# Three pieces of work put in another order in the attention loop of a one-core attention and mixture-of-experts kernel

## The reference

```python
def reference(x, ctx_1024, g_xattn, g_ffn, ...):       # x, ctx: (32, 512, 512)
    x = x + tanh(g_xattn) * xattn(layernorm(x), ctx, ctx, ...)
    x = x + tanh(g_ffn) * ffn(layernorm(x), ...)

def xattn(q, k, v, ...):                               # 8 heads of 64
    gi = concatenate([q, k, v], axis=-1)
    ig, fg = gi @ igate_w.T + igate_b, gi @ fgate_w.T + fgate_b     # by head and row
    cs = cumsum(log_sigmoid(fg))
    log_D = where(tril, cs[:, None] - cs[None, :], -inf) + ig[None, :]
    D = exp(log_D - max(log_D))
    C = (qh @ kh.T / sqrt(64)) * D
    h = (C / (maximum(abs(C.sum(-1)), exp(-max(log_D))) + 1e-6)) @ vh
    return (h - mean(h)) / sqrt(var(h) + 1e-5) * out_w              # by head

def ffn(x, ...):     # 8 experts, each takes its 2048 likeliest of 16384 rows
    ...
```

## Time and profile before

| | us |
|---|---|
| median of 3 runs | 3043.23 (3041.03 to 3049.25) |
| profiled execution, its own time | 3042.49 |
| its span, first to last instruction | 3040.7 |
| mean granted TensorE clock | 0.986 of 2.4 GHz |
| busy in the span: PE, DVE, ACT, POOL | 2903.3, 1824.0, 1073.1, 1064.0 |
| first stage, to the first instruction of the selection | 988.3 |

### The profile page before, as it was taken

How to read it: one execution, slowest core, us unless ns; L and a number is a source line. 1 busy time by engine, 2 the same in 40 slices (tenths; PEclk the granted TensorE clock), 3 DMA queues, 4 the chain that set the end, 5 groups by cost and what they waited for, 6 DMA issues and landing times.

```text
span 3040.7 us, 59653 instructions
## 1 busy us (share of the span) xinstructions
PE 2903.3 (95%) x24196; PEld 2342.4 (77%) x24196; DVE 1824.0 (60%) x5124; ACT 1073.1 (35%) x1897; POOL 1064.0 (35%) x1029
## 2 busy tenths in 40 slices
PE   6999999999997599999999999999999999999998
PEld 5777777777776477877877777787787787777886
DVE  6999999999997745344454444445535445444332
ACT  4777777777775211121211121122112112112110
POOL 4778777777785311211112111121112112121111
PEclk8999999999998799999999999999999999999999
DMA  5355554555543412231232132232123114222121
GB/s 176 130 196 175 190 183 168 197 185 179 195 163 113 127 34 38 56 75 31 54 95 51 31 80 38 37 100 55 34 36 98 35 33 110 37 51 57 35 37 24
DMA packets 157977, 284.18 MB, mean 93 GB/s; under 512 B 32992, under 2 KB 32992, under 8 KB 157704
## 3 DMA queue, kind: packets, MB, share of 16 engines
q1 hardware_dynamic: 123704, 204.36, 20.1%
q0 software_dynamic: 28672, 67.65, 12.6%
q10 hardware_dynamic: 5328, 8.36, 0.9%
HBM read 170.79 MB, written 101.19 MB: 89 GB/s over the span
## 4 chain that ended last, share of the span: by engine, by line
PE 63%; DMA 2%; DVE 2%; issue 0%; ACT 0%; POOL 0%; ACTq 0%; DVEq 0%; POOLq 0%
PE DN L1736 32%; PE UP L1707 30%; DMA w_raw<-in_L_ffn_W_down 2%; PE TT L1680 1%; DVE c_hit L1399 0%; DVE down_lo L1265 0%; PE c_bank L1392 0%; ACT z L1650 0%; PE c_bank L1376 0%; DVE c_hit L1420 0%; DVE c_within L1415 0%; ACT down_hi L1259 0%; POOL out_x L1625 0%; DVE mid_lo L1768 0%; DVE c_gained L1452 0%
## 5 line engine op out<-in xcount | busy, mean ns | idle before, releaser
L1625 POOL DMA_INDIRECT out_x<-y,slots x128 | 208.5, 1629 | 1622.3 <-DVE y L1792 1622.3
L1650 ACT ACTIVATE z<-UP,bup 128x512 f32<-128x512 f32 (+1 forms) x352 | 240.7, 686 | 1082.1 <-PE UP L1707 1060.5
L1736 PE MATMUL DN<-down_hi,mid_hi 128*128 128x512 f32 x1408 | 570.9, 405 | 0.0
L1707 PE MATMUL UP<-xT_hi,up_hi 128*128 128x512 f32 (+1 forms) x1408 | 553.8, 393 | 2.3 <-DVE xT_lo L1747 1.2
L1707 PE MATMUL UP<-xT_hi,up_lo 128*128 128x512 f32 (+1 forms) x1408 | 554.7, 394 | 0.0
L1707 PE MATMUL UP<-xT_lo,up_hi 128*128 128x512 f32 (+1 forms) x1408 | 551.4, 392 | 0.0
L1736 PE MATMUL DN<-down_hi,mid_lo 128*128 128x512 f32 x1280 | 505.8, 395 | 0.0
L1736 PE MATMUL DN<-down_lo,mid_hi 128*128 128x512 f32 x1280 | 505.7, 395 | 0.0
L1766 DVE CAST mid_hi<-z 128x512 fp32r<-128x512 f32 (+1 forms) x352 | 151.1, 429 | 483.4 <-ACT z L1650 483.4
L1790 DVE TENSOR_TENSOR y<-DN,bdn 128x512 f32<-128x512 f32 x128 | 88.5, 692 | 432.4 <-PE DN L1736 419.6
L1707 PEld LDWEIGHTS UP<-xT_hi,up_hi 128*128 128x128 f32 (+1 forms) x1408 | 259.9, 185 | 70.6 <-ACT z L1650 6.6
(11 more groups left out here) (258 smaller groups left out, 4754.6 us busy)
## 6 DMA issues: line engine op xcount, KB each, us to landing
xs<-in_x SPq DMA_DIRECT2D x64, 512.0 KB, 3.6
kraw<-in_ctx SPq DMA_DIRECT2D x32, 1024.0 KB, 6.5
kT<-in_ctx_by_feature SPq DMA_DIRECT2D x64, 512.0 KB, 5.6
out_x<-xs SPq DMA_DIRECT2D x32, 1024.0 KB, 11.2
rows_scratch<-xfb SPq DMA_DIRECT2D x32, 1024.0 KB, 9.1
w_raw<-in_L_ffn_W_down SPq DMA_DIRECT2D x40, 512.0 KB, 4.3
w_raw<-in_L_ffn_W_up SPq DMA_DIRECT2D x16, 682.5 KB, 4.2
mid_hi<-mid_hi ACTq DMA_DIRECT2D x32, 86.0 KB
```

Of the source, the lines that this page charges most:

```text
L1625: pool.indirect_dma_start(out_rows, bass.IndirectOffsetOnAxis(ap=slots[:, m:m + 1], axis=0), y[:, t, :], None, compute_op=ALU.add).then_in ...
L1650: act.activation(z[0:r, k % 2, :], UP[k % 3][0:r, :], ACT.Silu, bias=bup[0:r, e // 2, f:f + 1]).then_inc(s["z"], 1)
L1707: mm = pe.matmul(UP[k % 3][0:r, :], weights.up[wa][:, c, f * P:f * P + r], xT[xa][:, c, :], start=first, stop=(c == CH - 1 and wa == 1))
L1736: mm = pe.matmul(DN[m % 2][:, :], lhs, rhs, start=first, stop=(f == FCH - 1 and lhs is parts[-1][0]))
```

## The change

Three edits, none of which adds or removes an instruction. ACT computes the gates' logarithms ahead of the guess of the roots. DVE does the third pair's scores and the gate sums ahead of the roots. POOL weighs the values (`weigh_v`) ahead of all four `add_rows` instead of behind the first of them.

```diff
@@ POOL
                     if live(b3):
                         weigh_columns(step, pool, b3, slice(0, TILES))
+                        if live(b1):
+                            weigh_v(b1)
                         for j in range(TILES):
-                            if j == 1 and live(b1):
-                                weigh_v(b1)
                             ins = add_rows(pool, b3, j)
@@ ACT
-                    rsqrt_guess(i)
 
                     if live(b1):
                         log_sigmoid(b1)
+                    rsqrt_guess(i)
                     if live(b4):
                         second_norm(b4, (0,))
@@ DVE
                     row_variances(i)
                     if live(b2):
                         weighted_queries(b2, 2)
-                    reciprocal_roots(i)
-
-                    if live(b2):
                         weighted_scores(b2, 2)
                     if live(b1):
                         gate_runs(b1)
+                    reciprocal_roots(i)
                     if live(b2):
                         weighted_queries(b2, 3)
```

## The result

| | before, same chip | after |
|---|---|---|
| median, us | 3045.81 (3041.03 to 3049.25) | 3155.22 (3151.63 to 3161.80) |
| ratio, 95% interval | | 1.035 [1.033, 1.0369] |
| profiled execution, us | 3042.49 | 3152.79 |
| mean granted TensorE clock | 0.986 | 0.961 |

A forecast was written before the change was run, and what follows sets the result against it. It took the first stage's round to close over DVE and POOL together, with 0.37 us of slack. 28 rounds at 1.76 us (49.3) plus the other rounds made +53.1 on 3042.5: 3095 us, 8-in-10 range 3076 to 3126.

The forecast's parts named there:

- V to R: DVE, start of `vv` (V) to end of `nn` (R, roots): V + 3.94 if nothing waits, V + 4.42 if shift product binds.
- ACT's hold: ACT's chunk totals queue behind the second normalisation, which needs the roots: `prior` at R + 2.25, 1.84 us later in the round.
- POOL's holds: DVE's L949 and L964 held to the end of POOL instructions: L949 to R + 9.04, L964 to R + 22.57.
- the round of 30.70: Forecast length of a steady round of the first stage's loop, 1.76 us more than before.
- without the hold it is ... 30.60: The round if L964 is not held by POOL and the shift product binds: 26.18 + 4.42 = 30.60 us.
- the clock falls as well: Rival, chance 0.20: PE's stand of about 2 us lowers its clock; round 31.75, total 3125 us.
- the last of the signs of a wrong forecast: Granted clock below 1.00 showing in many windows between 110 and 900 us.
- The hidden hold: Rival, chance 0.07: chunk totals ready in time, only POOL late and holding DVE; round at least 29.70, total 3067 us.
- The ends: Rounds 1 to 3, the step from 3 to 4, and rounds 32 and 33: 3.8 us beside the 28 steady rounds.

The follow-up runs named there:

- totals first: The changed kernel with all three edits, and ACT's chunk totals moved ahead of the second normalisation of the first tile: 3095.71 us, 1.016.
- the scores first: The changed kernel with PE's 16 products of the fourth pair's scores written ahead of the chunk ends instead of behind them: 3101.56 us, 1.0164.
- the rows turned first: The kernel before, none of the three edits, with PE's second turn of the normalised rows (L693) ahead of the second pair's scores (L761): 3089.27 us, 1.0136.

## Why the prediction was wrong

**V to R: right.** R was given as V + 3.94 to V + 4.42. It is V + 4.43 in after, with `rise` waiting for the shift product, and V + 3.93 (548.73 - 544.80) where the hold at the end of the round covers that.

**ACT's hold: right in place, with one time that holds at the full clock only.** L557 stands behind L526 and `prior` was put at R + 2.25; with the clock held it is R + 2.28 (551.01 - 548.73). In after it is R + 2.69, since L736 and L737 run at half clock.

**POOL's holds and the round of 30.70: right at the full clock.** There the fourth L394 ends 22.50 behind R and L964 is held to R + 22.55, for R + 22.57 forecast; the round is 30.67. The alternative that the sum gives "without the hold it is ... 30.60" was measured too: 30.62. That the two cases lie so close was in the sum, and means that neither cause can be given a share of the 1.7 us. The rule of the Trainium skill ("SBUF — State Buffer", section "Who interferes with whom") that a DVE instruction with two SBUF inputs is held for the whole of a POOL instruction that reads SBUF says that L965 can be held like L964, and the trace with totals first agrees: 0.97 us instead of 0.21.

**The step that failed: that the clock would hold.** The case "the clock falls as well" had a chance of 0.20, on the ground that before had "one such fall in the rows". That ground was none: from 200 to 860 us before has no wait of PE over 1.1 us, so its rows say nothing of a wait of 2 us once a round, and in the one stretch of its steady rounds where the clock did fall, PE had stood 1.36 of 4 us, no single wait of it over 0.96. In after it falls in every round, which is the last of the signs of a wrong forecast that the prediction names. With PE's wait filled and its order kept, the rounds whose clock holds last 30.67 us, for 30.70 forecast; after's last 32.75. So some 2.1 us a round, 56 of the 109 us over the 27 rounds, go with the fall of the clock, and most of the rest is what the forecast had. The time of 3101.56 with the scores first lies near the forecast's 3095 too, but in part by luck: two falls there cost nothing, and a few rounds are longer by stops of another kind.

**That case was also priced too low**, at a round of 31.75, near after's shorter rounds of 32.0 but not its mean. The price took 1.7 us of PE's work from one window of the earlier trace rows. In the round of 33.09 that is shown, one of the longer ones, the two windows lose 3.4 us of clock ((0.39 + 0.47) x 4). The price let L949 be held to the end of one more L242, at R + 10.19; it is not held, and ends at R + 11.03 (580.03 - 569.00): `prior` is 0.44 later than R + 2.25, and the way from there to L949's end is 8.34 instead of 6.60, 1.64 of that the wait at L1099. These 0.84 us and the 0.47 by which L949 to L964 is longer (13.21 instead of 12.74, with the 0.39 of `gb`) make up nearly all of the 1.34 between 31.75 and 33.09. What a fall costs is not one figure: nothing in rounds 13 and 15 with the scores first, 0.3 us with totals first (30.7 against 30.39), 0.9 with the rows turned first, 1.3 to 2.7 in after (32.0 to 33.4 against 30.67).

**The hidden hold** (29.70 a round) had 0.07. With the totals first it gave 30.39 at best. L949 met POOL's second L242 and L964 was held to the end of the third L394, both as said; DVE's wait of 0.55 for the second pair's scores (L761) brought L964 later but not past that end. What the price left out is that L965 behind it is held too, to the end of the fourth: 0.97 us instead of 0.21, 0.76 more, where 30.39 is 0.69 longer than 29.70. The prediction had such a hold behind L964 "in round 4 alone here".

**The ends** were put at 3.8 us beside 28 rounds, 4 to 31. These 28 take 104.6 us more (101.5 and 3.1 of round 31), so the ends are 5.7 (110.3 - 104.6), nearly all of it in round 32, which took 4.9 more where 1.7 was put.

## What to carry to other kernels

When a step is put behind a slower one on its engine, follow every engine that waits for it, in its own order: here ACT's `second_norm` took the chunk totals with it, and PE stood behind them. Where TensorE runs at its full clock, price a new wait there by what a fall of the clock costs the readers of its next products too, and look first for work of TensorE's own to put into the wait. After each edit list TensorE's waits again, since a new one may have taken the old one's place. Where two loops close within a few tenths of a microsecond of each other, an experiment that removes one of them shows little (0.28 and 0.05 us of the round here, against 0.70 for both); remove both. Filling a wait with work that changes nothing else separates the clock from the order; moving real work into it does not.

## What was not expected of the hardware

The granted clock fell to about half in every round of after, where PE stood some 2.1 us once a round of 32.75 and, in the round shown, was busy right up to it; and in every round with ACT's and POOL's edits, where it mostly stood 1.5 to 1.6. The Trainium skill ("TensorE: Matmul & The Clock Gate", section "HAM oscillation — how this bites in real kernels") describes such an oscillation for products that wait for transfers, with longer waits than these; here a wait for another engine's small instruction did it. Yet the length of the wait does not settle it. With totals first PE waits for POOL's `climb` in 23 of the 27 rounds, 1.25 us in all but one, and the clock falls right behind it in 15 of these and holds in eight. With the scores first, 1.07 us in after's place, it fell behind that wait in rounds 13 and 15 and held in nearly all others. POOL's edit alone has PE wait 1.08 us before L761 in every round, and the clock never fell behind that. With the rows turned first it fell behind 0.51 us in 12 rounds. What tells those apart from the rounds that kept their clock stays open.
